# A small mixing and dequantized linear kernel: scale and zero rows spread by TensorE, and another order of the first loads, the weight unpacking and the first four tiles

## What is computed

```python
W = weights[condition]                       # (64, 64, 64), one of 16 matrices for each batch entry
y = einsum('bct,bcd->bdt', x, W)             # x: (64, 64, 1024)
v0, v1 = p[:, :, 0] & 63, p[:, :, 0] >> 6 & 63
v2, v3 = p[:, :, 1] & 63, p[:, :, 2] & 63    # p: (1024, 256, 3) int32 words
w = (stack([v0, v1, v2, v3]).reshape(1024, 1024) - zero_point) * scale   # both (1024, 1)
out = x + einsum('bsk,nk->bsn', y, w) + bias
```

## Time and profile before

| | us |
|---|---|
| median of 3 runs (lowest to highest) | 305.54 (304.91 to 306.17) |
| time of the profiled execution | 306.89 |
| its span | 304.6 |
| PE busy in the span | 290.2 (95%) |
| DVE, POOL, ACT busy | 193.0, 89.9, 77.8 |

### The profile page before, as it was taken

How to read it: one execution, slowest core, us unless ns; L and a number is a source line. 1 busy time by engine, 2 the same in 40 slices (tenths; PEclk the granted TensorE clock), 3 DMA queues, 4 the chain that set the end, 5 groups by cost and what they waited for, 6 DMA issues and landing times.

```text
span 304.6 us, 8374 instructions
## 1 busy us (share of the span) xinstructions
PE 290.2 (95%) x3236; PEld 241.8 (79%) x3236; DVE 193.0 (63%) x261; ACT 77.8 (26%) x169; POOL 89.9 (30%) x39
## 2 busy tenths in 40 slices
PE   8796499999999999999999999999999999999995
PEld 3674377888888888888888888888888888888885
DVE  3669985566566756566566756566566756566554
ACT  3664123332140505031140505031140505020000
POOL 1007503640424343340424343340414343330000
PEclk9899589999999999999999999999999999999999
DMA  6993055544152434424152424424252421111221
GB/s 209 281 384 113 4 166 194 169 139 166 71 183 103 131 118 140 144 83 167 69 189 95 146 103 141 143 100 150 76 189 89 176 74 69 69 70 39 90 82 69
DMA packets 20689, 39.54 MB, mean 130 GB/s; under 512 B 6850, under 2 KB 7106, under 8 KB 20674
## 3 DMA queue, kind: packets, MB, share of 16 engines
q1 hardware_dynamic: 20674, 39.33, 37.2%
HBM read 22.54 MB, written 16.78 MB: 129 GB/s over the span
## 4 chain that ended last, share of the span: by engine, by line
PE 90%; DVE 5%; SPq 2%; DMA 2%; issue 1%; ACT 0%; DVEq 0%
PE o_ps L299 76%; PE y_ps L262 10%; PE ysum_ps L276 2%; DMA q_raw<-in_L_ffn_qweight_dram 2%; DVE q_int L446 1%; DVE q_int L448 1%; DVE q_bf L455 1%; DVE q_int L450 1%; PE o_ps L284 1%; PE y_ps L299 1%; SPq L175 0%; DVE y_lo L463 0%; SPq L146 0%; SPq L142 0%; ACT junk L370 0%
## 5 line engine op out<-in xcount | busy, mean ns | idle before, releaser
L299 PE MATMUL o_ps<-qT,y_hi 128*128 128x512 f32 (+1 forms) x512 | 201.7, 394 | 0.0
L299 PE MATMUL o_ps<-qT,y_lo 128*128 128x512 f32 (+1 forms) x512 | 199.4, 390 | 0.0
L573 POOL TENSOR_TENSOR resid<-x_sb,bias_bc 128x1024 f32<-128x1024 f32 x32 | 88.7, 2776 | 182.9 <-DVE o_sb L491 160.1
L299 PEld LDWEIGHTS o_ps<-qT,y_hi 128*128 128x128 f32 x512 | 97.1, 190 | 20.5
L299 PEld LDWEIGHTS o_ps<-qT,y_lo 128*128 128x128 f32 x512 | 97.1, 190 | 19.5
L483 DVE TENSOR_TENSOR o_sb<-o_ps,scale_bc 128x512 f32<-128x512 f32 x63 | 43.6, 692 | 84.8 <-PE o_ps L299 84.8
L379 ACT ACTIVATE y_hi<-y_ps 128x512 fp32r<-128x512 f32 x64 | 33.4, 603 | 180.1 <-PE y_ps L262 180.1
L491 DVE TENSOR_TENSOR o_sb<-o_sb,resid 128x512 f32<-128x512 f32 x63 | 48.5, 770 | 2.7 <-DVE resid L472 0.5
L463 DVE TENSOR_TENSOR y_lo<-y_ps,y_hi 128x512 fp32r<-128x512 f32 x64 | 40.0, 684 | 11.6 <-ACT y_hi L379 11.6
L472 DVE SCALAR_TENSOR_TENSOR resid<-zs_bc,ysum,resid 128x1024 f32<-128x1024 f32 x32 | 40.9, 1277 | 0.0
L370 ACT ACTIVATE junk<-x_sb 128x1024 bf16<-128x1024 f32 x32 | 34.1, 1089 | 4.0 <-DMA x_sb<-in_x_dram 4.0
(11 more groups left out here) (25 smaller groups left out, 44.0 us busy)
## 6 DMA issues: line engine op xcount, KB each, us to landing
x_sb<-in_x_dram SPq DMA_DIRECT2D x32, 512.0 KB, 3.4
out_dram<-o_sb SPq DMA_DIRECT2D x63, 256.0 KB, 2.1
q_raw<-in_L_ffn_qweight_dram SPq DMA_DIRECT2D x8, 384.0 KB, 5.7
w_sb<-in_L_cond_weights_dram SPq DMA_DIRECT2D x64, 16.0 KB, 2.0
scale_bc<-_L_ffn_weight_scale_dram SPq DMA_DIRECT2D x1, 512.0 KB, 7.5
zs_bc<-n_weight_zero_point_dram SPq DMA_DIRECT2D x1, 512.0 KB, 7.8
bias_bc<-in_L_ffn_bias_dram SPq DMA_DIRECT2D x1, 512.0 KB, 8.6
out_dram<-o_sb SPq DMA_DIRECT2D x2, 128.0 KB, 1.9
```

The costliest lines, as they stand in the source:

```text
L299: last = nc.tensor.matmul(bank, part[:, slot, kt, :], qT[:, kt, col:col + width], start=(kt == 0 and part is y_hi), stop=(kt == KT - 1 and ...
L573: nc.gpsimd.tensor_tensor(resid[:, j % RING, :], x_sb[:, j % RING, :], bias_bc[:], ALU.add).then_inc(xbias_ready, 1)
```

## The change

1. `scale` and `zero` are loaded as single rows of 4 KB, issued by ACT, with blocks 1 and 2 of the weight. PE spreads each row over 128 partitions by four float32 matmuls of a row of ones by 512 columns (`spread`), into PSUM banks that are free then. ACT copies the scale to `scale_bc`; DVE computes `zs_bc` from the zero in one operation for each half (`place_zs`), where two operations of 1024 stood. The sign goes into `copy_ysum` (scale -1).
2. `unpack_q` loses its fourth operation: PE transposes the int16 bits as they are, and `place_q` reads them as int16 and subtracts 32. `q_int` has four buffers.
3. PE's, ACT's, DVE's and SP's lists of the start are written in another order, and the first `linear` is cut into pieces of 256 columns. `sum_y` waits for the copy of the sums before it. The matmuls on zeros go from 20 to 5. The stores of tile 0's second half and the reload of tile 6 change places.
4. POOL's sums wait until all eight blocks are unpacked. Loop and end are otherwise as they were.

The core of the diff:

```diff
-WARMUP = 20
+WARMUP = 5
...
+        scale_ps = [y_ps[:, 1, 0, :, :].rearrange("p t r -> p (t r)"), o_ps[:, 0, :]]
+        zero_ps = [y_ps[:, 1, h, :, :].rearrange("p t r -> p (t r)") for h in range(H)]
...
+        def load_row(eng, row, src, s):
+            eng.dma_start(row[:], src.rearrange("n a -> a n")).then_inc(s, 16)
...
             sp.dma_start(ids[:], cond.rearrange("(a b) -> a b", a=1)).then_inc(ids_loaded, 16)
+            load_q(sp, 0)
             load_x(0, 0)
-            load_q(0)
-            load_q(1)
...
             load_w(0, 0)
+            load_q(sp, 3)
             load_x(1, 0)
-            load_q(2)
-            load_q(3)
             load_w(1, 0)
-            load_row(scale_bc, scale.rearrange("n a -> (n a)"), scale_loaded)
+            for n in range(4, NT):
+                load_q(sp, n)
+            sp.dma_start(bias_bc[:], bias.partition_broadcast(P)).then_inc(bias_loaded, 16)
             load_x(2, 0)
-            load_q(4)
             load_w(2, 0)
-            for n in range(5, NT):
-                load_q(n)
-            load_row(zs_bc, zero.rearrange("n a -> (n a)"), zero_loaded)
-            load_row(bias_bc, bias, bias_loaded)
...
-                if not isinstance(t, int) or t >= RING:
-                    pe.wait_ge(ysum_ready, t - RING + 1)
+                if not isinstance(t, int) or t >= 1:
+                    pe.wait_ge(ysum_ready, t - paired)
...
-                pe.wait_ge(q_cast, n + 1)
+                pe.wait_ge(q_part, 3 * (n + 1))
...
+            def spread(bank, row, h):
+                nc.tensor.matmul(bank, ones[:], row[:, h * NH:(h + 1) * NH],
+                                 start=True, stop=True).then_inc(row_ps_ready, 1)
...
+            keep_warm(WARMUP)
+            pe.wait_ge(ones_ready, 1)
+            pe.wait_ge(scale_loaded, 16)
+            spread(scale_ps[0], scale_row, 0)
+            pe.wait_ge(ident_ready, 1)
+            transpose_q(0)
+            spread(scale_ps[1], scale_row, 1)
+            transpose_q(1)
             wait_mix(0, 0)
             mix(0, 0)
-            sum_y(0, 0)
-            pe.wait_ge(ident_ready, 1)
-            for n in range(NT // 2):
-                transpose_q(n)
+            transpose_q(2)
+            pe.wait_ge(zero_loaded, 16)
+            pe.wait_ge(scale_ready, 1)
+            for h in range(H):
+                spread(zero_ps[h], zero_row, h)
+            transpose_q(3)
+            pe.wait_ge(scale_ready, 2)
+            pe.wait_ge(qt_ready, 2)
+            pe.wait_ge(y_hi_ready, 2)
+            products(o_ps[:, 0, 0:2 * P], 0, 2 * P, 0, parts=(y_hi,))
+            wait_linear(0, 0, 0)
+            products(o_ps[:, 0, 0:2 * P], 0, 2 * P, 0, parts=(y_lo,))
+            pe.wait_ge(zs_ready, 2)
             wait_mix(1, 0)
             mix(1, 0)
-            pe.wait_ge(qt_ready, NT // 2)
-            linear(0, 0, 0)
+            transpose_q(4)
+            pe.wait_ge(qt_ready, 4)
+            products(o_ps[:, 0, 2 * P:NH], 2 * P, NH - 2 * P, 0).then_inc(o_ps_ready[0], 1)
+            transpose_q(5)
+            sum_y(0, 0)
+            transpose_q(6)
+            wait_linear(1, 0, 0)
+            products(o_ps[:, 0, :], 0, NH, 1, range(KT // 2))
+            transpose_q(7)
+            products(o_ps[:, 0, :], 0, NH, 1, range(KT // 2, KT)).then_inc(o_ps_ready[0], 1)
             sum_y(1, 0)
             wait_mix(2, 0)
             mix(2, 0)
+            pe.wait_ge(qt_ready, NT)
+            linear(0, 0, 1)
             sum_y(2, 0)
-            transpose_q(4)
-            transpose_q(5)
-            linear(1, 0, 0)
-            transpose_q(6)
-            transpose_q(7)
             linear(2, 0, 0)
...
+            load_row(act, scale_row, scale, scale_loaded)
+            load_row(act, zero_row, zero, zero_loaded)
+            load_q(act, 1)
+            load_q(act, 2)
...
-                dve.wait_ge(q_part, 3 * (n + 1))
-                if n >= 4:
-                    dve.wait_ge(qt_ps_ready, n - 3)
-                nc.vector.tensor_scalar(q_bf[:, n % 4, :], to.rearrange("p g j -> p (g j)"), QCENTER, None,
-                                        ALU.subtract).then_inc(q_cast, 1)
...
+            def place_zs(h):
+                cols = slice(h * NH, (h + 1) * NH)
+                dve.wait_ge(row_ps_ready, 2 + h + 1)
+                dve.wait_ge(scale_ready, h + 1)
+                nc.vector.scalar_tensor_tensor(zs_bc[:, cols], zero_ps[h], QCENTER, scale_bc[:, cols],
+                                               ALU.subtract, ALU.mult).then_inc(zs_ready, 1)
...
             pool.wait_ge(bias_loaded, 16)
+            pool.wait_ge(q_part, 3 * NT)
```

More of the change, by code:

```diff
@@ L70, in adaln_ffn @@
         q_raw = sb("q_raw", [P, NT, KP], I32)
-        q_int = sb("q_int", [P, 2, G, 4], I16)
-        q_bf = sb("q_bf", [P, 4, K], BF16)
+        q_int = sb("q_int", [P, 4, G, 4], I16)
         ident = sb("ident", [P, P], BF16)
+        scale_row = sb("scale_row", [1, N], F32)
+        zero_row = sb("zero_row", [1, N], F32)
+        ones = sb("ones", [1, P], F32)
         scale_bc = sb("scale_bc", [P, N], F32)
@@ L106, in adaln_ffn @@
         ident_ready = sem("ident_ready")
-        zs_part = sem("zs_part")
+        ones_ready = sem("ones_ready")
+        row_ps_ready = sem("row_ps_ready")
+        scale_ready = sem("scale_ready")
+        zs_ready = sem("zs_ready")
         q_part = sem("q_part")
-        q_cast = sem("q_cast")
         qt_ps_ready = sem("qt_ps_ready")
@@ L130, in x_arrived, with load_q @@
             eng.wait_ge(x_loaded[j % RING], (i + j // RING + 1) * 16)
+        def load_q(eng, n):
+            eng.dma_start(q_raw[:, n, :], qweight[n * P:(n + 1) * P, :]).then_inc(q_loaded[n], 16)
+        def load_row(eng, row, src, s):
+            eng.dma_start(row[:], src.rearrange("n a -> a n")).then_inc(s, 16)
         @block.sync
@@ L266, in mix, with sum_y @@
                                 last.then_inc(y_ps_ready, 1)
-            def sum_y(j, i):
+            def sum_y(j, i, paired=0):
                 t = i * RING + j
@@ L283, in transpose_q, with wait_linear @@
                 for kt in range(KT):
-                    last = nc.tensor.transpose(qt_banks[n % 2][:, kt, :], q_bf[:, n % 4, kt * P:(kt + 1) * P],
+                    last = nc.tensor.transpose(qt_banks[n % 2][:, kt, :], q_cols[:, n % 4, kt * P:(kt + 1) * P],
                                                ident[:])
                 last.then_inc(qt_ps_ready, 1)
-            def linear(j, i, h):
+            def wait_linear(j, i, h):
                 t = i * RING + j
@@ L293, in linear, with products @@
                     pe.wait_ge(scaled[h], t)
+            def linear(j, i, h):
+                wait_linear(j, i, h)
                 products(o_ps[:, h, :], h * NH, NH, j % RING).then_inc(o_ps_ready[h], 1)
-            def products(bank, col, width, slot):
-                for kt in range(KT):
-                    for part in (y_hi, y_lo):
+            def products(bank, col, width, slot, kts=range(KT), parts=(y_hi, y_lo)):
+                for kt in kts:
+                    for part in parts:
                         last = nc.tensor.matmul(bank, part[:, slot, kt, :], qT[:, kt, col:col + width],
@@ L307, in step @@
                         wait_mix(j + LEAD, i)
-                    for j in pair:
-                        sum_y(j + LEAD, i)
+                    for paired, j in enumerate(pair):
+                        sum_y(j + LEAD, i, paired)
                     for j in pair:
@@ L314, in step, with keep_warm @@
                         linear(j, i, h)
-            pe.wait_ge(warm_ready, 1)
-            for _ in range(WARMUP):
-                nc.tensor.matmul(ysum_ps[:], warm[:, 0:P], warm[:], start=True, stop=True)
+            def keep_warm(times):
+                for _ in range(times):
+                    nc.tensor.matmul(ysum_ps[:], warm[:, 0:P], warm[:], start=True, stop=True)
+            def spread(bank, row, h):
+                nc.tensor.matmul(bank, ones[:], row[:, h * NH:(h + 1) * NH],
+                                 start=True, stop=True).then_inc(row_ps_ready, 1)
+            pe.wait_ge(warm_ready, 1)
+            keep_warm(WARMUP)
[6 more added lines that the diff above has]
+            transpose_q(1)
             wait_mix(0, 0)
             mix(0, 0)
-            sum_y(0, 0)
-            pe.wait_ge(ident_ready, 1)
-            for n in range(NT // 2):
-                transpose_q(n)
+            transpose_q(2)
[11 more added lines that the diff above has]
+            pe.wait_ge(zs_ready, 2)
             wait_mix(1, 0)
             mix(1, 0)
-            pe.wait_ge(qt_ready, NT // 2)
-            linear(0, 0, 0)
+            transpose_q(4)
[8 more added lines that the diff above has]
+            products(o_ps[:, 0, :], 0, NH, 1, range(KT // 2, KT)).then_inc(o_ps_ready[0], 1)
             sum_y(1, 0)
@@ L342, in _ @@
             sum_y(3, 0)
[L343 to L349, removed]
+            linear(1, 0, 1)
+            wait_mix(4, 0)
```

(59 more changed lines are left out.)

14 lines of the change are left out of this document (6 added, 8 removed).

## The result

The changed kernel took 301.07 us (median of 4 runs, 298.62 to 301.11) against 305.65: ratio 0.983, 95% interval 0.980 to 0.986. Faster, as forecast, and beyond the noise, but by 4.6 us (1.5%) where 12.4 were expected; 301.07 lies above the range of 290.0 to 297.5. Three of the four executions took 301.0 to 301.1 and one 298.62; the experiments come back to that difference. The profiled execution took 301.04, its span 299.1 (before 306.89 and 304.6).

A forecast was written before the change was run, and what follows sets the result against it. PE sets the end, with its losses in the start. Zeros 3.3 + work 42.5 + spreads 4.1 + clock 1.5 + waits 0.6 = 52.0 us against 64.41; 305.54 - 12.4 = 293.1 us, range 290.0 to 297.5.

The forecast's parts named there:

- the 7.35 us gap: Start of the old kernel: PE waits at 34.81 for the last block of weights, behind DVE's slow int16 operations.
- the fast int16 operations: DVE's unpacking in the start: int16 operations near 0.46 us throughout, where four had taken 2.42 to 2.59.
- rows that land in time: Start: the 4 KB row load was taken as 2 us, landing at about 3 us.
- the moment when the zeros end: PE's opening: five matmuls on zeros from 1.17, at 0.43 us each, end at 3.3 us.
- ACT's and SP's lists: Start: first matrices land near 7.3 for PE at 7.8; ACT's last `place_q` ends near 22.1, needed at 24.2.
- Low clock at the start: PE's start: 1.2 GHz level from 3.3 to 6.2 us, 1.5 us lost; bounds nothing to about 4.
- the opening: First term of PE's list: five matmuls on zeros, over at 3.3 us.
- The waits that stay: PE's start: waits for scale row, block 0 and hand-overs between ACT, DVE and PE; 0.6 us, between 0 and 3.
- the collision: Rival, chance 0.12: POOL's sums meet DVE's residuals, tile 0's second half is scaled late; price 0 to 2.4, 295.5 us.
- The late opening: Rival, chance 0.25: at the start 2 us of wait and 2 of clock, total 297 us.
- a first mix after 9 us: Start of PE's list: the sign named for the rival of 2 us wait and 2 of clock, chance 0.25.
- The row load as a slow transfer: Rival, chance 0.03: `scale_row` moves element by element in 90 us, PE starts near 91, total about 381 us.

## Why the prediction was wrong

**Right:** the place (all in the start; the loop kept its length), the end of the 7.35 us gap, the fast int16 operations, rows that land in time, the moment when the zeros end (3.48 for 3.3), and ACT's and SP's lists, for which PE waited nowhere.

**The step that failed** is the term "Low clock at the start": I took the moment at which the clock rose in the kernel before, 6.2 us, and so 1.5 us lost. In the profiled execution it rose at about 20.7. What that cost can be read from equal work: from the first spread to the end of the first 16 + 16 matmuls of 256 columns, the list took 20.73 us (3.48 to 24.21), and with 20 zeros 14.36 (7.11 to 21.47), of which 1.5 was that run's own low stretch. So 7.9 us were lost, 6.4 more than the term and about twice its upper bound of 4. (Half of the low time, 8.6, is a little too much, as a mix goes from 1.92 to 1.09 and not to half.) The sum then closes: 52.0 + 6.4 for the clock, + 0.5 for the waits, + 0.2 for the opening, - 0.1 for the spreads is 59.0, where the loop began at 58.88.

The error was to carry over a time of rise from an opening of dense matmuls to one whose work had been exchanged. I priced the spreads only by their columns, 4.1 us (they took 7.70 at the low level and 4.0 at the high one, so that term was good), and missed what may happen to the clock around them. The runs show a fall of the clock behind thin spreads in five of six profiles (in the sixth it was low already) and behind full ones in none of three. By the times of the executions, the rise at 20 us occurred only with thin ones. Three things stay open: why the clock rose at 20 us in some executions and at 11 to 12 in others of the same program; whether the later start of work has a part in the early rise of the runs without thin spreads; and what the transposes of small integers, whose bits PE now reads as bf16, do, though they are in the runs with full rows and without spreads too.

**The waits that stay** were 0.6 us in the sum; the collision took 1.08 by itself. It was a rival with 0.12, priced at up to 2.4, and its mechanism was right: each addition ended 0.5 to 0.6 us behind the POOL sum beside it. The Trainium skill (SBUF — State Buffer, on the shared port pair) has a GpSimd operation that reads SBUF and a DVE operation with two SBUF inputs lock each other out for a whole instruction, and the additions of 2.70 and 2.18 us agree. (The int16 rows that the prediction offered for it show no operation with two SBUF inputs, as each of them has one.) Its place was 46 instead of 33 us, and the scaling that came late was that of tile 1's second half, not tile 0's. I also said the hold costs nothing, being a wait that ends earlier than the old start; because the clock made everything 7 us later, POOL started at 26.0, not before 24.79.

**The late opening** had the low clock in it, at 2 us, and blamed the loads for it. Its sign, a first mix after 9 us, came up for another reason: PE waited for no load, and the mix began at 9.4 because the list ahead of it ran at half speed. The x tile did take 5.3 us to land, where it took 3.1 before. By the Trainium skill (DMA: Bandwidth & Descriptors, "Issuing engines are not separate DMA queues") it shares the engines with ACT's blocks, and the trace agrees as far as it goes; but it now stands behind block 0 on SP's queue too, and no run separates the two. It cost nothing. The row load as a slow transfer is refuted: PE left the zeros at 3.48 with the row there.

## What to carry to other kernels

When a change alters what TensorE does in its first microseconds, do not carry over the moment at which its clock rose before: give the term bounds that cover the whole start, and read it from equal instructions at both levels rather than from the clock column. Repeat the run, since one program can have two times. A matmul with one row in use is not free filler: the same spreads with zeros in the other 127 rows took no longer, and with 20 zeros the kernel gained 2 us. And a contention that is moved away from one engine's list must be looked for in the next thing that list does: the hold alone gained nothing.

## What the runs showed of the hardware that I had not expected

- PE was busy without a gap for 17 us at the 1.2 GHz level (3.48 to 20.49, 8 transposes in 0.97 us), while the clock column says 1.00.
- Repeats of one program differ by 3 us (301.1 against 298.3). In the two that were profiled, all of it lies in when the clock was high before 25 us.
- A float32 matmul of 512 columns, two instructions in the profile, took 0.95 to 1.05 us at the high level with one row in use, and 0.86 to 0.91 with 128 (20 zeros).
- A DVE addition that takes 0.69 us alone took 2.70 beside POOL's sums, and ended 0.5 us behind the sum that was running.
